# A decoder layer on one core: batch 0's feed-forward moved into the last cross-attention groups, batch 1's tail cut into halves of 256 tokens

## The reference

```
x = x + causal self-attention(norm(x))            16 heads of 64
x = x + differential cross-attention(norm(x), ctx) 16 heads, two softmaxes each:
        a1 - lam * a2, times v, times 0.2, then @ out_proj.T + bias
x = x + feed-forward(norm(x)):
        act_quant(x)  @ weight_quant(w1).T         per token: round(x * 127/max|x|)
        depthwise conv over tokens (3 taps) + conv bias, silu     hidden width 512
        act_quant(h)  @ weight_quant(w2).T
```

## Time and profile before

| | |
|---|---|
| median of 3 runs | 341.22 us (337.72 to 343.09) |
| profiled execution | 343.06 us, span 341.2 us, mean granted TensorE clock 0.932 |
| busy | PE 301.1 us (88%), DVE 225.1 (66%), ACT 206.1 (60%), POOL 120.0 (35%) |
| chain that ended last | PE 70%, DVE 14%, ACT 10%, issue 4% |

### The profile page before, as it was taken

How to read it: one execution, slowest core, us unless ns; L and a number is a source line. 1 busy time by engine, 2 the same in 40 slices (tenths; PEclk the granted TensorE clock), 3 DMA queues, 4 the chain that set the end, 5 groups by cost and what they waited for, 6 DMA issues and landing times.

```text
span 341.2 us, 6666 instructions
## 1 busy us (share of the span) xinstructions
PE 301.1 (88%) x2486; PEld 186.3 (55%) x2486; DVE 225.1 (66%) x504; ACT 206.1 (60%) x496; POOL 120.0 (35%) x194
## 2 busy tenths in 40 slices
PE   1697889899999989898999997999998879987794
PEld 0464766566666686565666663354444333355562
DVE  3844577987777706785777489478888763078554
ACT  2466457667777724966778318477776474345254
POOL 3624527884477814834464000333240000000000
PEclk9999599999999999999999999599999795789698
DMA  7900000000000000000000000000000000000001
GB/s 284 318 11 1 2 1 2 3 2 2 1 2 3 2 0 2 3 0 2 2 2 2 2 0 2 0 1 2 0 2 1 3 0 0 0 2 0 0 25 39
DMA packets 4834, 6.18 MB, mean 18 GB/s; under 512 B 833, under 2 KB 3649, under 8 KB 4674
## 3 DMA queue, kind: packets, MB, share of 16 engines
q1 hardware_dynamic: 4514, 5.42, 4.5%
q10 hardware_dynamic: 288, 0.33, 0.3%
HBM read 5.23 MB, written 0.52 MB: 17 GB/s over the span
## 4 chain that ended last, share of the span: by engine, by line
PE 70%; DVE 14%; ACT 10%; issue 4%; DMA 1%; ACTq 0%; DVEq 0%
PE bank L604 62%; PE bank L677 5%; ACT pr L425 4%; DVE nmax L1163 3%; ACT pT L425 1%; DVE qk L1208 1%; PE bank L731 1%; DVE xn L1107 1%; ACT pT L522 1%; DVE stats L1094 1%; DMA x_sb<-in_x 1%; DVE onT L1333 1%; ACT L522 1%; DVE rx L1327 1%; ACT L383 1%
## 5 line engine op out<-in xcount | busy, mean ns | idle before, releaser
L522 ACT ACTIVATE pT<-bank 128x512 f32<-128x512 f32 (+1 forms) x80 | 44.4, 600 | 30.1 <-PE bank L604 29.8
L1208 DVE TENSOR_REDUCE qk<-bank 128x4 fp32r<-128x616 f32 x64 | 49.2, 795 | 19.8 <-PE bank L604 19.7
L309 POOL TENSOR_SCALAR pr<-pr,pinv 128x256 f32<-128x256 f32 (+2 forms) x96 | 46.0, 496 | 33.5 <-DVE pinv L1171 33.4
L425 ACT ACTIVATE pr<-bank,nmax 128x256 f32<-128x256 f32 (+2 forms) x96 | 44.3, 478 | 20.6 <-DVE nmax L1163 20.4
L604 PE MATMUL bank<-qs 64*128 64x256 f32 (+3 forms) x256 | 49.4, 469 | 3.7 <-ACT pr L425 3.7
L1163 DVE TENSOR_REDUCE nmax<-bank 128x2 f32<-128x512 f32 (+2 forms) x48 | 31.6, 686 | 14.9 <-PE bank L604 14.8
L604 PE MATMUL bank<-pT,v_sb 128*64 128x128 f32 (+2 forms) x320 | 38.4, 385 | 0.0
L319 POOL TENSOR_TENSOR km<-kb_,con 128x1232 fp32r<-128x1232 f32 x8 | 18.0, 2246 | 52.2 <-PE bank L604 50.2
L604 PE MATMUL bank<-qk,km 64*128 64x512 f32 x64 | 29.7, 481 | 5.2 <-ACT pT L522 5.2
L309 POOL TENSOR_SCALAR pT<-pT,pinv 128x512 f32<-128x512 f32 x32 | 21.7, 692 | 30.3 <-DVE pinv L1171 30.3
L604 PE MATMUL bank<-km,qk 64*128 64x308 f32 x128 | 29.8, 380 | 1.6 <-DVE qk L1208 1.5
(11 more groups left out here) (161 smaller groups left out, 580.9 us busy)
## 6 DMA issues: line engine op xcount, KB each, us to landing
pT<-in_wqk SPq DMA_DIRECT2D x1, 1024.0 KB, 6.2
cw_sb<-in_cw SPq DMA_DIRECT2D x1, 768.0 KB, 8.7
x_sb<-in_x SPq DMA_DIRECT2D x2, 256.0 KB, 5.2
pT<-in_wv SPq DMA_DIRECT2D x1, 512.0 KB, 6.9
wo_sb<-in_wo SPq DMA_DIRECT2D x1, 512.0 KB, 7.1
out<-x_sb SPq DMA_DIRECT2D x8, 64.0 KB, 1.5
onT<-in_consts ACTq DMA_DIRECT2D x1, 256.0 KB, 6.5
pT<-in_xwk SPq DMA_DIRECT2D x1, 256.0 KB, 7.4
```

The lines of the kernel that those rows point to most:

```text
L309: nc.gpsimd.tensor_scalar(d, d, pinv[:, t, a:a + 1], 1.0, ALU.mult, ALU.mult).then_inc(norm_done, 1)
L425: nc.scalar.activation(prob[r][:, a, at:at + w], bank[:, SP[k % 2] + a, at:at + w], ACT.Exp, bias=nmax[:, t, a:a + 1], accum_out=psum[:, t ...
L522: nc.scalar.activation(px[rows, i, :], bank[rows, (ST0, ST1)[i % 2], :], ACT.Exp, scale=SD ** -0.5).then_inc(xexp_done, 1)
L1208: nc.vector.tensor_reduce(m, s_in, AX.X, ALU.max, negate=True).then_inc(round_done, 1)
```

## The change

Names and line numbers of the changed kernel's own rows differ from the profile's; the functions keep their names.

1. **Batch 0 earlier.** `turn_sums`/`combine` of batch 0 go from group 5 (four rounds) to group 4 (two rounds of 256 tokens, with 128x128 transposes in place of 64x64). Transposes and projection go to group 5, where the projection is a round of its own. The rows of the projection's weight come in their plain order. Square root, centring and scales go to group 6.
2. **Batch 0's convolution in group 7.** conv(0) stands tap by tap between the last scores of group 7, conv(1) around the last weighted sums and `turn_sums` of batch 1.
3. **Batch 1 in halves.** `turn_att`, `cross_out`, residual, statistics, root, scales, quantisation, `turn_ints` and the splitting run for 256 tokens and then for the other 256. conv(4) needs the first half alone, conv(5) both.
4. **Work moved to POOL:** norm_apply of batch 1 (group 0), the query rows of groups 6 and 7, the joining of batch 0's heads, quantising batch 0's tokens, and rounding tiles 0 to 6 of the hidden layer with its factor.
5. **Scales without the norm.** Rows are centred alone; rstd goes into the token scale, so the absolute maximum can be taken before the root is there.
6. **Bias as one two-row matmul**, placed first in conv instead of two one-row matmuls placed last.
7. **Hidden integers.** `hidden_ints` is gone: the f32 numbers are transposed (four f32 transposes into a whole bank), and the copy out subtracts the rounding constant. `down` has one bank instead of two.
8. The loop over tiles runs `down(i-5)`, `turn_hidden(i-4)`, `conv(i)`; four hidden tiles stand behind conv(7) instead of three.

```diff
-SUMS_AFTER_ROUND = {1: 0, 3: 1, 5: 2, 7: 3}
+SUMS_AFTER_ROUND = {5: 0, 7: 1}
+HALF = NT // 2
+CONV_BANK = (SM, SM + 1, OB, ST0)
+HIDDEN_BANK = (PT, ST1)
 @block.gpsimd
+            norm_apply(1)
             for g in range(NG):
                 spread_keys(NG + g)
 ...
             add_cross_bias(1)
+            query_rows(6)
+            join_heads(0)
+            join_heads(1)
+            query_rows(7)
+            bias_rows()
+            quantise_tokens()
+            for i in range(TT - 1):
+                quantise_hidden(i)
 @block.scalar
             for G in range(B * NG):
 ...
+                if G == 6:
+                    root_of_variance(0, 5)
+                if G == 5:
+                    turned_att(1, whole)
+                if G == 7:
+                    act.wait_ge(zero_done, 3)
+                    turned_ints(1, 0, whole)
                 cross_exps(G, range(4, 7))
 ...
                 cross_exps(G, range(7, 10))
-                if G == 6:
-                    root_of_variance(0, 5)
             copy_sums(B * NG - 1)
+            turned_att(2, halves[0])
+            turned_att(3, halves[1])
+            root_of_half(0)
+            root_of_half(1)
             silu(0)
             silu(1)
+            turned_ints(2, 1, halves[0])
             silu(2)
             turned_hidden(0)
+            turned_ints(3, 1, halves[1])
             silu(3)
+            turned_hidden(1)
+            for i in range(4, TT):
+                silu(i)
                 turned_hidden(i - 2)
 @block.tensor
             def conv(i, taps=range(3)):
 ...
+                    mm(o, ones_row[0:2, :], cb_h[0:2], True, False)
                 for k in taps:
 ...
-                    mm(o, ones_row[0:1, :], cb_h[0:1], False, False)
-                    mm(o, ones_row[0:1, :], cb_l[0:1], False, True).then_inc(conv_ps, 1)
+                    last.then_inc(conv_ps, 1)
             def down(i):
                 pe.wait_ge(hiT_done, i + 1)
+                if i == 0:
+                    pe.wait_ge(xo_done, 2)
+                else:
+                    pe.wait_ge(f_done, i)
 ...
-            for i in range(TT):
-                if i == 1:
-                    turn_ints(1)
-                if i + 3 < TT:
-                    conv(i + 3)
+            turn_ints(1, first)
+            conv(4, [0])
+            turn_hidden(0)
+            conv(4, [1, 2])
+            turn_ints(1, second)
+            down(0)
+            turn_hidden(1)
+            conv(5)
+            for i in range(6, TT):
+                down(i - 5)
+                turn_hidden(i - 4)
+                conv(i)
+            for i in range(TT - 4, TT):
                 turn_hidden(i)
-                if i >= 1:
-                    down(i - 1)
+                down(i - 1)
             down(TT - 1)
 @block.vector
             for G in range(B * NG - 1):
 ...
+                    if G == 6 and j == 1:
+                        centre(range(NT))
+                    if G == 6 and j == 2:
+                        inverse_root(0, 5)
+                        token_scale(range(NT))
+                if G == 5:
+                    tile_stats(range(NT))
+            low_ints(1, 0, slice(0, T))
+            combine(1, 0)
+            combine(1, 1)
+            cross_residual(1, 0)
+            tile_stats(first)
+            cross_residual(1, 1)
+            tile_stats(second)
+            centre(first)
+            half_root(0)
+            token_scale(first)
+            quantise_tokens(0)
+            hidden_scale(0)
+            low_ints(2, 1, halves[0])
+            centre(second)
+            half_root(1)
+            token_scale(second)
+            quantise_tokens(1)
+            hidden_scale(1)
+            low_ints(3, 1, halves[1])
+            hidden_scale(2)
+            hidden_scale(3)
+            for i in range(4, TT):
+                finish(i - 4)
+                hidden_scale(i)
+            quantise_last()
+            for i in range(TT - 4, TT):
+                finish(i)
```

More of the change, by code:

```diff
@@ L555, in turned_hidden @@
                     act.wait_ge(f_ps, i - 1)
-                nc.scalar.copy(hiT[:, i % 2, :], bank[:, (SM, SM + 1)[i % 2], 0:FH // 2].bitcast(BF16)).then_inc(
-                    hiT_done, 1)
+                nc.scalar.activation(hiT[:, i % 2, :], bank[:, HIDDEN_BANK[i % 2], :], ACT.Identity,
+                                     bias=minus_round[:, :]).then_inc(hiT_done, 1)
+            whole, halves = slice(0, T), (slice(0, T // 2), slice(T // 2, T))
             for G in range(B * NG):
@@ L826, in turn_sums, with turn_att @@
                 last.then_inc(round_ps, 1)
-            def turn_att(b):
-                pe.wait_ge(att_done, NT * (b + 1))
-                for t in range(NT):
+            def turn_att(done, ts):
+                pe.wait_ge(att_done, done)
+                for t in ts:
                     last = nc.tensor.transpose(bank[:, PJ0, t * P:t * P + P], att[:, t, :], con[:, C_ID:C_ID + P])
                 last.then_inc(attT_ps, 1)
-            def cross_out(b):
-                pe.wait_ge(attT_done, b + 1)
-                for t in range(NT):
-                    last = mm(bank[:, PJ0, C * t:C * t + C], attT[:, t * P:t * P + P], xwo_sb[:, :], t == 0,
-                              t == NT - 1, skip_group_check=True)
-                last.then_inc(xo_ps, 1)
@@ L841, in turn_ints, with cross_out @@
-            def turn_ints(b):
-                pe.wait_ge(xd_done, NT * (b + 1))
-                for t in range(NT):
+            def cross_out(at, ts, done):
+                for t in ts:
+                    last = mm(bank[:, at, C * t:C * t + C], attT[:, t * P:t * P + P], xwo_sb[:, :], t == ts[0],
+                              t == ts[-1], skip_group_check=True)
+                last.then_inc(done, 1)
+            def turn_ints(b, ts):
+                pe.wait_ge(xd_done, NT * b + ts[-1] + 1)
+                for t in ts:
@@ L1026, in _ @@
                     turn_norm(1, 4, PJ0)
+                if G == 5:
+                    pe.wait_ge(xq_act, 16)
+                    turn_att(2, range(NT))
+                if G == 7:
+                    pe.wait_ge(qb1_done, 8)
+                    turn_ints(0, range(NT))
                 if more:
@@ L1033, in _ @@
                 cross_scores(G, 5)
-                if G == 6:
-                    cross_out(0)
-                if not more:
-                    turn_ints(0)
                 cross_weighted_rest(G)
@@ L1041, in _ @@
                     next_max(G, 5)
+                if G == 5:
+                    pe.wait_ge(attT_done, 1)
+                    cross_out(next_round(), range(NT), round_ps)
+                if G == 7:
+                    pe.wait_ge(wcs, 3)
+                    pe.wait_ge(ones_done, 4)
+                    pe.wait_ge(round_done, rounds[0])
+                    conv(0, [0])
                 cross_scores(G, 7)
-                if G == 6:
-                    pe.wait_ge(xo_done, 1)
                 if more:
                     turn_cross_max(G + 1, reduced)
+                else:
+                    conv(0, [1])
                 cross_scores(G, 8)
@@ L1335, in combine @@
                                         ALU.mult).then_inc(round_done, 1)
+                if b == 0:
+                    return
                 dve.wait_ge(round_done, rounds[0])
[L1337 to L1341 removed]
```

386 lines of the change are left out of this document (232 added, 154 removed).

## The result

| | before | changed |
|---|---|---|
| median | 342.45 us (337.72 to 343.09, 12 runs) | **340.07 us** (338.58 to 341.17, 12 runs) |
| ratio | | **0.9951, 95% interval 0.9927 to 0.9975** |
| profiled execution, span | 343.06, 341.2 | 340.07, 338.3 |
| mean granted clock | 0.932 | 0.945 |
| busy PE, DVE, ACT, POOL | 301.1, 225.1, 206.1, 120.0 | 298.5, 214.6, 200.9, 141.5 |

The change takes 2.4 us off (by the ratio 1.7), where 6.6 were forecast. The sign was right; the size was not. The span of the profiled executions shows 2.9. Ratios use fast runs alone, those within 1.5% of the fastest of the same kernel in the same comparison; as the kernel before spreads from 337.0 to 346.9 us, ratios of different comparisons can be set against each other to about 0.5% only.

What follows compares the result with a forecast made beforehand. PE was taken to bound group 4, DVE group 5 and batch 1's chain, with the low clock after PE stops a separate cost. Gains 0.2 + 1.4 + 5.5 + 0 - 0.5 = 6.6 us gave 334.6 us, range 328.5 to 341.5.

Steps and rivals of the forecast that it cites:

- groups 4 and 5: Combine of batch 0 moved into group 4: 22.7 us together against 22.9, gain 0.2, from +1.1 to -1.5.
- group 6 to T0: Group 6 to batch 1's first transposed sums (T0): 28.9 us against 30.3, gain 1.4, between 4.7 and -10.2.
- T0 to conv(5): Batch 1's chain in halves: conv(5) 19.3 us behind batch 1's first transposed sums instead of 24.8, gain 5.5.
- from conv(7) on: Ending with four hidden tiles instead of three: 6.4 us to the last finish against 5.9, so -0.5.
- second rival: Groups give the gain back through group 4's rounds, late POOL query rows and collisions: 338.3 us, chance 0.23.
- the fourth: Move buys nothing because batch 1's chain waits on PE in place of DVE: 340 us, chance 0.04.
- group 6 to the end of PE's last stop: From group 6's start until PE gets the maxima of j = 2: 7.3 us, PE idle 3.4 of them.
- rest of group 6 at full clock: Group 6 work left after PE's stop: 7.2 us at full clock less 2.9 done, so 4.3.
- group 7 to T0 at full clock: Group 7 from score 2, two scores, conv(0), conv(1)'s bias and two taps, eight transposes: 12.3 us.
- what the low level adds: Low clock after group 6's stop lasts 10.1 us, halving 5.0 us of work; bounds 1.7 and 16.6.
- first rival: Clock recovers sooner: low level lasts 3.4 us in group 6 and conv(4) runs at full; 329.8 us, chance 0.21.
- The third: Low level holds from group 6's stop to batch 1's first transposed sums: 346.2 us, slower than before, chance 0.07.

Runs made afterwards that it cites:

- e2: Changed kernel with an exponential in place of batch 0's square root in group 6, so no table load there: 335.21 us, ratio 0.9833.
- e5: Changed kernel with 11 extra dense matmuls, results unread, where PE stands still in group 6; loads and root stay: 333.08 us, ratio 0.9721.
- e8: Changed kernel with fillers in group 6 and before batch 1's first-half integers, plus two banks for down: 331.25 us, ratio 0.9649.
- e1: Changed kernel with 14 extra dense matmuls, results unread, in PE's wait for batch 1's first-half integers ahead of conv(4): 339.11 us, ratio 0.999.
- e6: Changed kernel with batch 1's four tiles centred, quantised, transposed and split at once instead of in halves: 345.43 us, ratio 1.0043.
- e4: Changed kernel with two banks in turn for down instead of one: 338.59 us, ratio 0.9945.
- e7: Changed kernel with batch 0's root back at the end of group 6, reciprocal and scales behind it on DVE: 343.69 us, ratio 1.0006.
- e3: Changed kernel with conv(0) in one piece behind group 7's last score instead of taps between scores: 342.78 us, ratio 1.0016.
- e11: Changed kernel with fillers in group 6 and ahead of conv(4) and two banks for down, rerun on another kernel's chip: 331.52 us, ratio 0.9704.

## Why the prediction came out as it did

Against the sum, term by term, on the profiled executions:

| step | forecast | measured | gain forecast | gain measured |
|---|---|---|---|---|
| groups 4 and 5 | 12.3 + 10.4 | 12.5 + 10.5 | +0.2 | -0.1 |
| group 6 to T0 | 28.9 | 30.6 | +1.4 | -0.3 |
| T0 to conv(5) | 19.3 | 20.5 | +5.5 | +4.3 |
| conv(5) to conv(7) | no change | 6.80 for 6.75 | 0 | -0.05 |
| from conv(7) on | 0.5 longer | 11.95 for 10.8 | -0.5 | -1.15 |
| start of group 4 | same | 0.2 earlier | 0 | +0.2 |
| sum | | | 6.6 | 2.9 |

**Groups 4 and 5: right.** Twelve and ten us, as worked out from the earlier trace rows. POOL's query rows came at 250.7 and PE asked at 250.8, so the 0 held, by 0.16 us. The second rival (the groups give the gain back) gives a time near the result, and the fourth (the move buys nothing, 340) gives the very result, but neither is how the time was lost: the groups cost what they were forecast to, and the chain behind T0 brought conv(4) at 13.46 us for 13.5.

**Group 6 to T0: the step that failed, by size.** It is the term of 12.3 us for the work of group 7 up to T0. The forecast's own terms, with what the runs show for each:

| term | forecast | measured |
|---|---|---|
| group 6 to the end of PE's last stop | 7.3 | 8.2 |
| rest of group 6 at full clock | 4.3 | 3.1 (e2, e5) |
| group 7 to T0 at full clock | 12.3 | 15.3 (e2, e5, e8) |
| what the low level adds | 5.0 | 4.0, the remainder of 30.6 |

PE's stops (3.12 us against 3.4) and the length of the low level (10.2 against 10.1) were as forecast. The second term rests on a slip of 1.0 us: 7.3 us with 3.4 of idle time hold 3.9 of work, and 2.9 was taken off. PE's work in group 6 was 8.17 us (e2) and not 7.2, so these two errors nearly cancel, as do the misses of the first two rows (0.9 too little, 1.2 too much). That the sum is off by only 1.7 us is partly luck: 3.0 too little in the third row against 1.0 too much in the fourth. These are rows of PE in the changed kernel, between two scores:

```profile
291.21 0.50 PE L679 MATMUL bank<-qk,wqk_h 128*128 128x512 f32 x1
291.55 0.39 PE L679 MATMUL bank<-qk,wqk_l 128*128 128x512 f32 x1
291.78 0.40 PE L679 MATMUL bank<-qk,wqk_h 128*128 128x512 f32 x1
292.10 0.49 PE L679 MATMUL bank<-qk,km 64*128 64x512 f32 x1
292.53 0.49 PE L679 MATMUL bank<-qk,wqk_h 128*128 128x512 f32 x1
```

A tap takes 0.89 us from its start to the score behind it, and a score 0.42 or 0.43. Before, nine such matmuls in a stream ran from 295.37 to 297.65, which is 0.76 a tap. conv(0) with its bias came to 3.10 us instead of the 2.5 that I took (2.28 and a bias of 0.42 would have been 2.70 by themselves), three scores to 0.3 more, and conv(1)'s bias and two taps to 2.12 for 1.65. PE also waited 0.69 us for ACT at the start of group 7, which I had at 0, and the first two scores in front of that wait (0.5) were in no term. That is 0.6 + 0.3 + 0.5 + 0.7 + 0.5 = 2.6 of the 3.0. The other 0.4 is in the 12.9 us at the low level, which were halved to 6.3: not all thin work takes double there (a pair of scores 1.28 us at 283.01, and 0.98 at full clock in e2). That would also be why 10.2 us at the low level cost 4.0 us and not half; no run takes the two apart.

**T0 to conv(5): mechanism right, size off by 1.2.** conv(4) came 13.46 us behind T0, for 13.5; conv(4) to conv(5) took 7.1 us for 5.8. The low level was sized from the 3.4 us of the earlier trace rows, and that is a part of it only. Before, it had already begun at 315, in the wait for the integers, and held for 6.8 us there too; in the changed kernel it holds for the same 6.8 us, but PE has work in nearly all of them. The stretch ahead of the earlier trace rows's in the kernel before, then conv(4) of the changed one:

```profile
315.00:318.70 3.70, 1.12 (x4) 0.72 (x4) 3.45 (x13) 1.75 (x3) 0.00 (x0) 0.54 0.00 0
```

```profile
312.50:318.40 5.90, 5.90 (x16) 4.38 (x17) 3.56 (x15) 1.28 (x2) 1.51 (x4) 0.50 0.00 0
```

Half of 5.9 is 2.95 us in place of 1.7, and that is the 1.2. PE has no wait for POOL in the changed kernel here. At full clock one appears: conv(4) to conv(5) takes 5.4 us in e1 and e8 and not the 4.1 that the forecast's 5.8 holds without its 1.7 for the clock, because POOL's rounding of tile 1 is then late by 1.1. That the halves are what gains is shown by e6.

**The ending: right in sign, 0.65 too small.** I named the wait of `down` for `finish` behind `quantise_last` and sized it too low; e4 takes 1.1 us of it away.

**The clock.** The forecast took the low stretch in group 6 as a given. That was the likelier case and it happened, but I asked only how long it would last. The larger question was how to stay out of it: e5 shows 3.8 us from G6 to T0 alone, more than the whole measured effect of the change. My first rival (the clock recovers soon, 329.8) did not happen: in group 6 the level lasted 10.2 us, and conv(4) ran at it. That e8 comes near its price with 331.25 is chance, as e8 has 1.1 us from a second bank too. The third did not happen either; e7 comes close to it.

**Table loads.** In the rows of ACT above each load starts 0.02 us behind the instruction ahead of it, the root starts 0.01 us behind its load, and the exponentials 0.02 behind theirs. The Trainium skill ("ScalarE: Activation LUTs", What ACT_TABLE_LOAD costs) adds a drain of about 1.38 us to each switch. By that page, an estimate, two switches would take 5.3 us of ACT; here the loads and the root take 2.8, from 273.18 to 275.97. The trace does not agree with the rule here.

**What stays open.** Why the low level lasts 3.4, 6.8, 10.2, 13.7 or 27.3 us, and why it begins behind a stop in one run and not in another: behind the same two stops of group 6 (0.34 and 0.84 to 0.86) it began in e1 and e7 and not in the changed kernel, e2, e3 or e4. Even in the shared part, at 35 us, it lasts 3.4, 6.8 or 10.2 us from run to run. Behind waits filled with dense matmuls it was absent in all six profiles that have such (e1, e5, e8 to e11), but that is one profile of each. Group 0's stretch was left as it is.

## What to carry over

Where a profile shows the clock falling behind a wait, price the wait with the low stretch that follows it, and first try cheap dense matmuls into a free bank inside the wait: here this was worth about 2% in the kernel before and 2 to 3% in the changed one (e8's 3% with a second bank in it), and the restructuring 0.5% by itself and about 1% with fillers in both. Read the whole low stretch, not only the part in which PE works. A step that runs at the low clock hides waits behind it, as e1 showed, so a gain worked out at full clock must look for the engine that is late next. When small pieces are woven between others, take their length from woven rows, not from a stream.
